# Second spectral mixer of a four-block network on one NeuronCore: another turn order, PSUM banks dealt anew

## What is computed

```
pooled  = x.mean(axis=(1, 2))
h       = mlp_scale * jnp.square(jax.nn.relu(pooled @ fc1_w)) + mlp_bias
routeing = softmax((h @ fc2_w).reshape(B, nf, med), axis=1)
xp = act1_scale * jnp.square(jax.nn.relu(x @ pwconv1_w)) + act1_bias
xf = rfft2(xp, axes=(1, 2), norm='ortho')
weight = einsum('bfc,hwf->bhwc', routeing, wc)
xo = irfft2(xf * weight, s=(H, W), axes=(1, 2), norm='ortho')
return xo @ pwconv2_w
```

## Time and profile before

| | us |
|---|---|
| median of 3 runs | 1007.01 |
| lowest, highest | 1004.34, 1007.79 |
| profiled execution | 1005.84 |
| its span | 1004.0 |
| TensorE matmul busy | 852.4 (85%) |
| VectorE busy | 633.5 (63%) |
| ScalarE busy | 454.8 (45%) |
| GpSimd busy | 561.0 (56%) |

### The profile page before, as it was taken

One profiled execution on the slowest core, in us unless ns is written; L12 is line 12 of the kernel. 1 busy time (PEld: TensorE's weight loads), 2 busy tenths in 40 slices (PEclk: granted clock), 3 DMA queues, 4 the chain that ended last, 5 costly groups with the idle time before them and its releaser, 6 DMA issues.

```text
span 1004.0 us, 24216 instructions
## 1 busy us (share of the span) xinstructions
PE 852.4 (85%) x8782; PEld 706.1 (70%) x8782; DVE 633.5 (63%) x1753; ACT 454.8 (45%) x892; POOL 561.0 (56%) x903
## 2 busy tenths in 40 slices
PE   4676767768889999969999699999868988999997
PEld 4455555647767888857888578888757777688876
DVE  5765778457775655666877536777635565367755
ACT  0433354146554444417766353444134554534441
POOL 5342452243417687866556257687714556576865
PEclk9877779579999999989999899999957898999999
DMA  8500010000012110000001000110000000101120
GB/s 177 101 17 0 9 32 1 1 1 1 1 48 64 34 40 24 25 2 1 0 0 40 25 25 26 39 34 25 2 1 1 1 1 27 47 25 39 34 72 17
DMA packets 39337, 26.58 MB, mean 26 GB/s; under 512 B 27320, under 2 KB 32041, under 8 KB 39201
## 3 DMA queue, kind: packets, MB, share of 16 engines
q1 hardware_dynamic: 38252, 24.64, 9.8%
q10 hardware_dynamic: 998, 0.80, 0.3%
HBM read 8.51 MB, written 1.57 MB: 10 GB/s over the span
## 4 chain that ended last, share of the span: by engine, by line
PE 61%; DVE 14%; ACT 8%; issue 8%; POOL 7%; DMA 1%; ACTq 0%; DVEq 0%; POOLq 0%
PE PS L1496 16%; PE PS L1469 7%; PE PS L1470 6%; PE PS L1473 4%; PE PS L1575 3%; PE PS L1412 3%; PE PS L1596 3%; ACT H L588 2%; PE PS L1588 2%; PE PS L1284 2%; ACT H L675 2%; PE PS L1646 2%; PE PS L1270 1%; PE PS L1331 1%; DVE H L1181 1%
## 5 line engine op out<-in xcount | busy, mean ns | idle before, releaser
L630 ACT ACTIVATE H<-PS,B 128x512 f32<-128x512 f32 x288 | 176.9, 685 | 212.4 <-PE PS L1473 211.8
L1496 PE MATMUL PS<-M,H 128*64 128x96 f32 x4608 | 203.5, 249 | 8.2 <-DVE X L1111 8.2
L1496 PEld LDWEIGHTS PS<-M,H 128*64 128x64 f32 x4608 | 194.6, 138 | 19.1 <-DVE X L1111 8.8
L430 POOL TENSOR_TENSOR msum<-stats 128x4 f32<-128x4 f32 (+1 forms) x61 | 14.2, 233 | 324.5 <-DVE stats L787 287.6
L1111 DVE SCALAR_TENSOR_TENSOR X<-PS,G,X 128x96 f32<-128x96 f32 (+1 forms) x384 | 121.0, 317 | 77.3 <-PE PS L1496 66.7
L1470 PE MATMUL PS<-FHL,M1l 128*128 128x512 f32 x192 | 76.2, 397 | 0.0
L1469 PE MATMUL PS<-XH,M1h 128*128 128x512 f32 x192 | 76.2, 397 | 0.0
L474 POOL TENSOR_TENSOR ex<-euler,dl 128x16 f32<-128x16 f32 x24 | 69.8, 2909 | 7.6 <-DVE dl L1075 7.4
L466 POOL TENSOR_TENSOR PF<-G,B 128x1536 f32<-128x1536 f32 x24 | 66.1, 2756 | 10.2 <-DVE G L1102 10.2
L444 POOL TENSOR_TENSOR rs<-ve,half 128x4 f32<-128x4 f32 (+1 forms) x61 | 66.0, 1081 | 4.8
L555 ACT ACTIVATE XH<-PS 96x512 fp32r<-96x512 f32 x56 | 33.0, 589 | 54.8 <-PE PS L1284 54.8
(11 more groups left out here) (246 smaller groups left out, 2004.4 us busy)
## 6 DMA issues: line engine op xcount, KB each, us to landing
FHL<-XH SPq DMA_DIRECT2D x36, 192.0 KB, 2.5
FHL<-XL SPq DMA_DIRECT2D x36, 64.0 KB, 2.2
X<-XH SPq DMA_DIRECT2D x12, 192.0 KB, 2.5
raw<-L_ffn_w SPq DMA_DIRECT2D x3, 576.0 KB, 4.9
M<-L_ffn_w SPq DMA_DIRECT2D x3, 576.0 KB, 6.1
X<-x SPq DMA_DIRECT2D x4, 384.0 KB, 6.7
XH<-XL SPq DMA_DIRECT2D x24, 64.0 KB, 1.9
out<-X SPq DMA_DIRECT2D x8, 192.0 KB, 2.5
```

The lines of the kernel that those rows point to most:

```text
L630: act.activation(H[p][:, c, :], bank(UB[c]), ACT.Gelu, bias=B1[e][:, c:c + 1]).then_inc(gelu_a, 1)
L1496: ins = pe.matmul(Y[rows, x * C:(x + 1) * C], H[p][:, j, t * P + rows.start:t * P + rows.stop], M2[e][:, j, :], start=c == 0, stop=c == CH ...
```

## The change

The banks are dealt anew. Weights use banks 0 and 1 twice in a body (`WB`), the second pair behind the products of the first. The spectra of one image (both channel halves) share one bank, 6 for image 0 and 4 for image 1 (`SB3`), and are copied out by one instruction of 512 columns (`mix_image`). The channel outputs of both images share bank 5 (`PB3`) and are copied out by one instruction (`mix_images_out`). `mix_tokens` goes to bank 2. The routing's transposes get bank 3 (`RTB`), so `prep_turn` waits only for the softmax's reading of the logits. `OF`, where GpSimd puts its sums, gets a second buffer. The turn order changes on all four engines. `moe(7, ...)` gets a wait for the last `mix_x` ahead of its first use of bank 2. ScalarE splits `mix_relu` in `mix_relu` and `mix_star`; the other mixer's functions lose their case for `kc == 1` and do as before.

```diff
         TB = bank(7, 512, C)
+        RTB = bank(3, 4 * C, NF)
...
-        DB, PB, IB = ((0, 4, 6, 5), (6, 0, 4, 2)), ((5, 1), (6, 4)), (3, 5)
+        DB, PB, IB = (0, 4, 6, 5), (5, 1), (3, 2)
+        WB, SB3, PB3, CWB = (0, 1, 0, 1), (6, 4), 5, (0, 1, 2, 6)
...
             def mixer3(g, p):
-                if has(g, 0):
-                    for n, j in enumerate(BY_IMAGE):
+                def sums(order):
+                    for n in order:
+                        j = BY_IMAGE[n]
                         pool.wait_ge(prod_v, 2 * (4 * g + n) + 2)
-                        pool.wait_ge(pp_pe, 16 + 2 * g)
-                        o = OF[0:C, j // 2, j % 2, :].rearrange("p (e r n) -> p e r n", e=2, r=2)
+                        pool.wait_ge(pp_pe, 14 + 2 * g)
+                        o = OF[p][0:C, j // 2, j % 2, :].rearrange("p (e r n) -> p e r n", e=2, r=2)
...
+                if has(g, 0):
+                    sums((0, 1))
                 if has(g, 3, 2, PREPS[6]):
                     prep(6, 5, g + 3)
+                if has(g, 0):
+                    sums((2, 3))
...
+            def mix_image(g, p, i):
+                act.wait_ge(dft_pe, 4 * (8 + g + 1) + 2 * i + 2)
+                after(act, prod_v, 8 * g)
+                act.activation(XF[1 - p][:, :, :, i, :], bank(SB3[i], 512, C).rearrange("p (c r f) -> p c r f", c=2, r=2), ACT.Copy)\
+                   .then_inc(xf_a, 2)
...
+            def mix_images_out(g):
+                act.wait_ge(pp_pe, 16 + 2 * g + 2)
+                act.wait_ge(id_pe, 8 + g)
+                act.activation(PF3, PS[:, PB3, 0:4 * C].rearrange("p (i n) -> p i n", i=2), ACT.Copy).then_inc(ps_a, 2)
...
                 if has(g, 1):
                     mix_relu(1, 5, g)
+                    mix_star(g, 0)
+                if has(g, 2, 2, PREPS[6]):
+                    prep_hi(40 + g + 2, p)
+                if has(g, -1):
+                    mix_images_out(g - 1)
+                if has(g, 1):
+                    mix_star(g, 1)
                 if has(g, 1, 2):
                     routing_hi(g + 1, 1 - p)
-                if has(g, -1):
-                    mix_out(1, g - 1)
-                if has(g, 2, 2, PREPS[6]):
-                    prep_hi(40 + g + 2, p)
                 if has(g, 1):
-                    mix_spectrum(1, g, p, (0, 1))
+                    mix_image(g, p, 0)
                 if has(g, 2, 2):
                     routing_relu(g + 2)
                 if has(g, 1):
-                    mix_spectrum(1, g, p, (2, 3))
+                    mix_image(g, p, 1)
...
                 if has(g, 1, 2):
+                    routing_max(g + 1)
+                if has(g, 3, 2, PREPS[6]):
+                    prep_stats(m + 3, g + 3, xu[5], xu[6])
+                if has(g, 1, 2):
                     routing_norm(g + 1)
-                if has(g, 1):
-                    mix_h(1, g)
                 if has(g, 0):
                     products((0, 1))
+                if has(g, 1):
+                    mix_halves(g, 0)
+                if prep:
+                    prep_lo(m + 2, p, g + 2 if has(g, 2, 2) else None)
+                if has(g, 0):
+                    products((2, 3))
+                if has(g, 1):
+                    mix_halves(g, 1)
+                if has(g, -1):
+                    mix_x(1, g - 1, xu[6])
                 if has(g, 1, 2):
                     routing_out(g + 1, 1 - p)
-                if has(g, 0):
-                    products((2, 3))
...
                 if has(g, 2, 2):
-                    routing(g + 2)
-            zero_rows(1, [OF])
+                    routing_star(g + 2)
+            zero_rows(1, OF)
...
             def mixer3(g, p):
...
                 if has(g, 1):
                     if has(g, 0):
-                        pe.wait_ge(xf_a, 32 + 4 * g + 2)
-                    if isinstance(g, int):
-                        after(pe, xu[6], g - 1)
+                        pe.wait_ge(xf_a, 32 + 4 * g + 4)
                     mix_h(1, 5, g, p)
                 if has(g, 0):
                     pe.wait_ge(rt_x, g + 1)
                     pe.wait_ge(xf_a, 32 + 4 * g + 4)
                     after(pe, prod_v, 8 * g)
-                    for j in BY_IMAGE:
-                        pe.matmul(bank(j, 8 * HF, C), RT[p][:, j, :], CWS[:], start=True, stop=True).then_inc(w_pe, 1)
+                    weights((0, 1))
+                if has(g, 2, 2, PREPS[6]):
+                    prep_turn(40 + g + 2, False, (rt_v, 5 * (g + 1 if has(g, 1) else GROUPS - 1) + 3))
                 if has(g, 1, 2):
                     route_turn(g + 1)
                 if has(g, -1):
                     if has(g, 1):
-                        pe.wait_ge(r_a, 2 * (8 + g + 1) + 1)
-                    mix_channels(1, g - 1)
-                    if has(g, 1):
                         pe.wait_ge(r_a, 2 * (8 + g + 1) + 2)
-                    else:
+                    mix_channels(1, g - 1, 1 - p)
+                if has(g, 0):
+                    pe.wait_ge(prod_v, 8 * g + 4)
+                    weights((2, 3))
+                if has(g, -1):
+                    if not has(g, 0):
                         pe.wait_ge(xu[6], g - 1)
                     mix_tokens(1, g - 1)
-                if has(g, 2, 2, PREPS[6]):
-                    prep_turn(40 + g + 2, False, (rt_x, g + 2 if has(g, 2, 2, 8) else GROUPS))
-                if has(g, 1):
-                    mix_dft(1, g, BY_IMAGE[:2])
                 if has(g, 2, 2):
                     route_in(g + 2, p)
                 if has(g, 1):
-                    mix_dft(1, g, BY_IMAGE[2:])
+                    mix_dft(1, g)
                 if has(g, 2, 2):
                     route_logits(g + 2)
             mixer_walk(pe, mixer3, GROUPS)
             pe.wait_ge(split_v, 22)
-            moe(7, 6, 2, -1)
+            moe(7, 6, 2, IB[1])
```

More of the change, by code:

```diff
@@ new lines, in mix_spectrum @@
+            def mix_spectrum(g, p):
+                for n, j in enumerate(BY_IMAGE):
+                    c, i = j // 2, j % 2
+                    act.wait_ge(dft_pe, 4 * g + 4 + n + 1)
+                    after(act, zx_p, 4 * g)
+                    for h in range(2):
+                        for r in range(2):
+                            ins = act.activation(XP[1 - p][64 * r:64 * r + 64, 2 * c + h, i, :],
+                                                 PS[64 * h:64 * h + 64, DB[j], r * FR:(r + 1) * FR], ACT.Copy)
+                    ins.then_inc(xf_a, 1)
@@ L702, in mixer2 @@
                 if has(g, -1):
-                    mix_out(0, g - 1)
+                    mix_out(g - 1)
                 if has(g, 0):
@@ L1166, in mixer2 @@
                 if has(g, 1):
-                    mix_h(0, g)
+                    mix_h(g)
                 if prep:
@@ L1224, in _ @@
             for i in range(2):
-                routing(i)
+                routing_star(i)
+                routing_max(i)
                 routing_norm(i)
@@ L1633, in _ @@
             for j in range(4):
-                pe.matmul(bank(j, 2 * HF, NF), cwv[:, :, j // 2], RB[:, (0, 1, 2, 2)[j], :], start=True, stop=True).then_inc(cw_pe, 1)
+                pe.matmul(bank(CWB[j], 2 * HF, NF), cwv[:, :, j // 2], RB[:, (0, 1, 2, 2)[j], :], start=True, stop=True).then_inc(cw_pe, 1)
             def route_in(i, p):
@@ L1662, in mixer3, with weights @@
             def mixer3(g, p):
+                def weights(order):
+                    for n in order:
+                        pe.matmul(bank(WB[n], 8 * HF, C), RT[p][:, BY_IMAGE[n], :], CWS[:], start=True, stop=True).then_inc(w_pe, 1)
                 if has(g, 1):
                     if has(g, 0):
-                        pe.wait_ge(xf_a, 32 + 4 * g + 2)
-                    if isinstance(g, int):
-                        after(pe, xu[6], g - 1)
+                        pe.wait_ge(xf_a, 32 + 4 * g + 4)
                     mix_h(1, 5, g, p)
```

112 lines of the change are left out of this document (42 added, 70 removed).

## The result

| | before (same chip) | after |
|---|---|---|
| median, us | 1007.4 of 4 | 996.63 of 4 |
| lowest, highest, us | 1004.34, 1008.97 | 994.24, 996.81 |
| ratio (95% interval) | | 0.9891 (0.9863 to 0.9919) |

The account below looks back on a forecast made before the run. TensorE was taken as nearest to a bound, standing still up to 2.65 us a body. Terms 0, -1.3, -6.8 and -3.2 gave -11.3 from 1005.84: 994.5, and 995 us for the median; range 987 to 1003.

Parts of the forecast that it names:

- Bodies -1 and 0: Start of the mixer: mix_h of body 0 about 2.3 us later, its 2.96 us wait shrinks; 0, between -1 and +1.
- Body 1: The mixer's body 1: from 14.25 to about 13.0 us with a like share of half clock, -1.3 (bounds -3.6 and -0.7).
- Bodies 2 to 5: Four mixer bodies: from 52.8 us to 4 x 11.5 = 46.0, -6.8 (bounds -10.4 and -3.6).
- The tail: From body 6 to the experts: from 23.06 to 19.9 us with one spell of half clock, -3.2 (bounds -4.8 and -1.5).
- The step that carries it: TensorE in each body: two waits totalling 2.65 us shrink to 0.6, so a full-clock body takes 10.6 instead of 12.9 us.
- The price of the clock: TensorE at 1.2 instead of 2.4 GHz: 3.5 us of half clock cost a new body the full 1.7 us, giving 12.3.
- Every second body: Mixer bodies: every second one taken as hit by half clock, 11.5 us on average between 10.6 and 12.3.
- The merged copies: ScalarE's channel-output copies: one of 384 columns takes 0.49 us, two of 192 take 0.55, so 0.06 gained on the path.
- A chain over ScalarE and VectorE: Rival: this chain paces the body through late products or softmax, 1.7 us more per body, 1004 us; chance 0.15.
- Its weak place: Second transforms in a body: image 1 needed at 7.75 us, ready from VectorE at 7.35, the narrowest place, 0.4 us.
- The slower rival, the clock: TensorE over the mixer: more, shorter stops keep it at 1.2 GHz; gain gone at 38 us of half clock; chance 0.07.
- the first rival: The chain over ScalarE and VectorE: terms become 0, -1 and -1.6, 1004 us; chance 0.15, half of it within 0.3%.

Follow-up runs that it names:

- early_zero: relu_first with VectorE clearing both OF buffers ahead of the first two groups' routing and taking group 2's statistics behind the halves in body -1: 990.89 us, ratio 0.9838.
- copy_late: The changed kernel with ScalarE copying the channel outputs behind image 1's square and scale and the routing's copies, as before: 1000.94 us, ratio 0.9939.
- copies_split: The changed kernel with each merged ScalarE copy (channel outputs, spectra of an image) split into two instructions again: 994.73 us, ratio 0.9859.
- relu_first: The changed kernel with ScalarE doing the routing's relu and square ahead of image 0's spectra copy: 990.43 us, ratio 0.9813.
- old_copy_early: The kernel before, with ScalarE copying both images' channel outputs directly behind the second relu, ahead of image 1's square and scale: 1039.49 us, ratio 1.0335.
- banks_only: The changed kernel's banks and merged copies, with the turn order of the kernel before on all four engines: 1015.07 us, ratio 1.0109.
- relu_first_again: A later run of the unchanged relu_first kernel, beside the changed kernel on the same chip: 991.53 us, ratio 0.9848.

## Why the prediction was right

**The total** was 995 and is 996.63; for the profiled execution 994.5 and 994.24. The sum was made of four terms, and their errors partly cancel.

- *Bodies -1 and 0*, taken at 0 between -1 and +1: they took 22.42 us instead of 21.95, and began 0.6 us later (744.41 against 743.81), a difference that the stages ahead of the mixer already show. Together +1.07 against before. Body -1 became 2.4 us longer and body 0 1.9 shorter, the shape that was laid out: body 0 waits for all four spectra, and its wait ahead of `route_in` of 2.96 is 1.11. Of the reasons given for the first, the wait for all four spectra is there (0.74 us ahead of body 0's `mix_h`). VectorE's clearing and statistics are not: early_zero takes them away and wins 0.06 us. What held it was ScalarE's new order, which the prediction left out at this place.
- *Body 1*, 13.0: 12.55, with 3.5 us of half clock instead of the like share of 5.4 that was assumed.
- *Bodies 2 to 5*, 46.0: 45.16. At full clock 10.75 to 10.93 where 10.6 was laid out; at half clock 12.56 where 12.3 was. What is too low is the wait ahead of the logits: 0.54, not 0.35, because the first transforms ended and image 0's copy began 8.24 us after `mix_h` (787.62), not 7.85, with the routing's relu behind it. What is too high is the number of half-clock bodies: one of these four (body 3), not two. These two errors, 0.15 to 0.33 us in each body one way and some 1.7 us once the other way, cancel in part, and that is luck.
- *The tail*, 19.9: 19.76.

**The step that carries it**, TensorE as the path once its two waits are gone, holds at full clock: body 5 gained 2.13 us where 2.3 was laid out. Of the waits 2.65 us became 0.8. The wait ahead of the inverse transform was forecast at 0.25 and is 0.25. The second weights don't wait in the loop (0.22 once, in body 0). copy_late puts back one of the two waits and gets it back in nearly its old size, where TensorE is at full clock. GpSimd, costed at nothing because its sums end in time, holds none of TensorE's stops directly; but it is not free, as the last section shows.

**The price of the clock.** "3.5 us of half clock cost the full 1.7": bodies 2 and 3 differ by 1.64, with 3.5 us of half clock between them. "Every second body" fits bodies 1, 3 and (with 3.6 us) 6, then misses 5. But no row spoke for it: in the kernel before, every body from 1 to 4 was hit, 22.7 us in all where 23 had been read. With every one hit in the new kernel too, the prediction's own figures give 49.2 us for bodies 2 to 5 instead of 46.0, and a total of 998 or more. That the half clock fell by half came close to what was assumed, and no run shows the reason. This part of the forecast is luck. The other eleven traces of the table have between 3.5 and 63.2 us of it.

**The merged copies**, 0.06 us on the path by the rows: 0.2 us over the whole sum between after and copies_split. The 1.7 us estimated by the 0.3 us for an instruction of the Trainium skill ("ScalarE: Activation LUTs", Rules for kernel authors) did not come.

**The rivals.** A chain over ScalarE and VectorE does not pace the body; its mark, a wait of a microsecond ahead of the second weights or the transforms, is nowhere in the loop. Its weak place is real, though: the second transforms' wait for image 1, with 0.4 us of slack by the layout, shows as 0.28 us in body 2 of relu_first, and old_copy_early is such a chain at work, in the old order. The slower rival, the clock, did not come: half clock fell from 22.7 to 10.6 us, and the mean over the mixer was 0.85 (0.82 before). banks_only shows that it is no empty fear: there the same banks with other stops nearly double the half clock. The rule of the Trainium skill weighed beside it ("TensorE: Matmul & The Clock Gate", A second HAM failure mode) agrees with this case only in that both levels alternate; fewer and shorter stops went with less half clock here, not more.

**Slips in the working.** Image 1's scale ends at 824.36 us, not at 824.24. With 1.7 us more per body the first rival's terms are +0.4, 0 and -1.6 and not 0, -1 and -1.6, so its time is 1006 and not 1004. Of its chance of 0.15, two thirds and not half were put within 0.3%. None of these changes the forecast.

## What to carry to other kernels

A turn order over four engines and a dealing of PSUM banks are one decision. Here the banks alone lose 7 us, one move of the order alone loses 31, and the whole new order with the new banks gains 11, part of each by the clock: before a copy is moved ahead of another step, ask what queues behind the step that is now late, and whether a shared bank ties that to TensorE. When TensorE has become the path, look at what stands in front of the smallest instruction that it waits for (a relu of 0.15 us behind a copy of 0.59), and judge such edits by distances between repeated starts in the trace, body by body and at like clock. They repeated to 0.01 us for the changed kernel, where whole times scatter by several; but two traces of relu_first differ by 1.5 us in the sum, so one trace is not enough.

## What was not expected of the hardware

The same VectorE instruction takes more or less time, by what GpSimd does meanwhile. VectorE and GpSimd in relu_first, one stretch of body 2, first VectorE's timeline, then GpSimd's:

```profile
785.28 0.41 DVE L1254 TENSOR_TENSOR H<-H,PS 96x256 f32<-96x256 f32 x1
785.61 0.88 DVE L1163 TENSOR_TENSOR H<-H 128x192 f32<-128x192 f32 x1
```

```profile
785.34 0.94 POOL L442 TENSOR_TENSOR XN<-X,mean 128x384 f32<-128x384 f32 x1
```

The add of image 1's halves, both inputs in SBUF, takes 0.88 us instead of 0.35 beside GpSimd's subtraction, while the product, with one input in PSUM, keeps its 0.41. That is no single case. In the kernel before, none of the 32 adds of halves meets a GpSimd instruction, and all take 0.35 to 0.36 us. In relu_first the 11 that meet only GpSimd instructions of a few columns take 0.34 to 0.36, and the 21 that meet a wide one (its sums of 128 columns or the 384 of the prepared input) take 0.35 to 0.98. The 32 products that meet a wide one take 0.41 to 0.42 all the same. Groups of instructions over the mixer, the second add of the halves in the kernels before, after and relu_first, one row each:

```profile
L1148 DVE TENSOR_TENSOR H<-H 128x192 f32<-128x192 f32 x12 | 4.2, 351 | 0.0
```

```profile
L1165 DVE TENSOR_TENSOR H<-H 128x192 f32<-128x192 f32 x12 | 5.1, 421 | 0.0
```

```profile
L1164 DVE TENSOR_TENSOR H<-H 128x192 f32<-128x192 f32 x12 | 5.9, 496 | 0.0
```

The mean goes from 351 to 421 to 496 ns: the two engines now meet, which in the kernel before they did not. GpSimd pays as well; its 64 sums of products go from 451 to 490 ns in the mean, which is 2.5 of its 4.9 us more. The trace agrees with the Trainium skill ("SBUF — State Buffer", Who interferes with whom), where a VectorE instruction with two SBUF inputs and a GpSimd instruction that reads SBUF share a pair of ports under an exclusive lock.

A like meeting explains the wait that relu_first leaves in bodies 3 and 5. In relu_first_again the routing's bias and scale (L1205, 24x2) take 0.28 us in body 2 and 0.75 in body 3. VectorE's timeline, both places:

```profile
786.25 0.28 DVE L1205 TENSOR_SCALAR hh<-hq,msb 24x2 f32<-24x2 f32 x1
...
796.88 0.75 DVE L1205 TENSOR_SCALAR hh<-hq,msb 24x2 f32<-24x2 f32 x1
```

GpSimd's, beside them:

```profile
786.10 1.04 POOL L446 TENSOR_TENSOR rs<-ve,half 128x4 f32<-128x4 f32 x1
...
796.79 0.83 POOL L448 TENSOR_TENSOR XN<-XN,rs 128x384 f32<-128x384 f32 x1
```

The short one lies beside GpSimd's power of 4 columns, the long one beside a scaling of 384 columns, and ends with it (797.63 and 797.62 us). In body 5 it is the same, 0.75 us beside that scaling. VectorE reaches this instruction 0.3 us later in body 3, where two of its adds had taken 0.61 and 0.76, and the logits wait for both. Bodies 2 and 3 are 0.7 us apart by this. Timing the two apart was not tried.
